# The edge phase's order keys replaced: where Pool's weights, VectorE's totals and comparisons stand in their queues

## What is computed

```
hi = x @ W1[:H];  hj = x @ W1[H:]
h = relu(hi[:, :, None, :] + hj[:, None, :, :] + b1)
y = layernorm(h @ W2 + b2) * gamma + beta
out = einsum('bij,bijh->bih', adj, y)
x = layernorm(x + out)
```

## Time and profile before

| | us |
|---|---|
| median of 3 runs | 449.18 (448.45 to 449.66) |
| the profiled launch, its time | 449.61 |
| its span, first to last instruction | 447.9 |
| TensorE (PE) busy | 429.5 |
| VectorE (DVE) busy | 422.7 |
| ScalarE (ACT) busy | 393.8 |
| Pool busy | 353.6 |

### The profile page before, as it was taken

The page is one execution under the profiler, slowest core; times in us unless marked ns, Lnnn a source line. Parts: engine busy times, 40 slices in busy tenths (PEclk is TensorE's granted clock), DMA queues, the critical chain, the costliest instruction groups (busy, mean ns, idle before and its releaser), DMA issues. The chain is left out here.

```text
span 447.9 us, 14059 instructions
## 1 busy us (share of the span) xinstructions
PE 429.5 (96%) x3391; PEld 403.8 (90%) x3391; DVE 422.7 (94%) x1555; ACT 393.8 (88%) x1001; POOL 353.6 (79%) x651
## 2 busy tenths in 40 slices
PE   7599989999999999999999999999999999999993
PEld 3599989999999999898999999999999999999992
DVE  6999999999999999998999999999999999999976
ACT  2378979999999899979899999999999999999994
POOL 3569979999999899953776878787878787878772
PEclk9989999999999999999999999999999999999998
DMA  6134334445444743232422223222323232323111
GB/s 225 43 86 124 101 127 159 154 157 159 155 157 152 240 162 120 80 129 78 136 89 73 88 66 92 66 92 64 94 64 94 64 94 63 95 65 97 59 37 50
DMA packets 50939, 47.60 MB, mean 106 GB/s; under 512 B 5584, under 2 KB 42576, under 8 KB 50896
## 3 DMA queue, kind: packets, MB, share of 16 engines
q1 hardware_dynamic: 49760, 46.45, 33.7%
q10 hardware_dynamic: 1136, 0.66, 0.5%
HBM read 28.22 MB, written 18.87 MB: 105 GB/s over the span
## 5 line engine op out<-in xcount | busy, mean ns | idle before, releaser
L1621 PE MATMUL bank<-w2c,hE 128*128 128x128 f32 x512 | 68.3, 277 | 0.4 <-ACT bank L928 0.4
L1621 PEld LDWEIGHTS bank<-w2c,hE 128*128 128x128 f32 x512 | 63.5, 192 | 2.6 <-issue 0.7
L1289 DVE TENSOR_TENSOR ym<-bank,wE 128x512 f32<-128x512 f32 x64 | 43.4, 684 | 4.3 <-POOL wE L775 3.3
L1264 DVE TENSOR_REDUCE ssum<-sqE 128x4 f32<-128x512 f32 x63 | 42.7, 678 | 3.0 <-ACT sqE L945 2.7
L1122 DVE BATCH_NORM_STATS2 stats<-t 128x6 f32<-128x128 f32 x192 | 44.5, 273 | 1.0 <-issue 1.0
L945 ACT ACTIVATE sqE<-bank 128x512 f32<-128x512 f32 x63 | 38.0, 603 | 8.0 <-PE bank L1621 8.0
L915 ACT ACTIVATE hE<-bank,front 128x512 f32<-128x512 f32 x64 | 43.5, 680 | 1.5 <-PE bank L1601 1.5
L742 POOL TENSOR_TENSOR half<-ym 128x512 f32<-128x512 f32 x31 | 39.6, 1276 | 5.7 <-DVE ym L1289 2.1
L775 POOL TENSOR_TENSOR wE<-erstd,fits 128x12 f32<-128x12 f32 x31 | 6.6, 213 | 44.8 <-DVE erstd L1278 44.8
L726 POOL TENSOR_TENSOR gHl<-gH,gHu 128x512 fp32r<-128x512 f32 x32 | 40.8, 1276 | 1.2 <-ACT gHu L899 1.2
L928 ACT ACTIVATE bank<-b2c 128x512 f32<-128x512 f32 x62 | 37.4, 604 | 0.5 <-DVE ym L1289 0.4
(11 more groups left out here) (192 smaller groups left out, 1643.6 us busy)
## 6 DMA issues: line engine op xcount, KB each, us to landing
hh_scratch<-hh SPq DMA_DIRECT2D x32, 256.0 KB, 2.2
gH<-hh_scratch SPq DMA_DIRECT2D x32, 256.0 KB, 2.7
A<-adj_groups SPq DMA_DIRECT2D x32, 128.0 KB, 2.1
res_scratch<-res SPq DMA_DIRECT2D x32, 128.0 KB, 2.0
gRES<-res_scratch SPq DMA_DIRECT2D x32, 128.0 KB, 2.0
AT<-adjT_groups SPq DMA_DIRECT2D x31, 128.0 KB, 2.2
out<-y SPq DMA_DIRECT2D x30, 128.0 KB, 1.8
X<-x_groups SPq DMA_DIRECT2D x29, 128.0 KB, 2.2
```

The source lines that it names most:

```text
L1264: nc.vector.tensor_reduce(ssum[q][:, g * ELL:(g + 1) * ELL], sqE[g][:, :, :], AX.X, ALU.add).then_inc(b[f"ssE{g}_ready"], 1)
L1289: nc.vector.tensor_tensor(ym[q][:, g, :, :], YE_ps[g], spread_last(wE[q][:, g * ELL:(g + 1) * ELL]), ALU.mult).then_inc(b[f"ymE{g}_ready"], 1)
L1621: last = nc.tensor.matmul(ps[:, i, :], hidden[:, i * P:(i + 1) * P], w2c[:, :], start=False, stop=i == tiles - 1, skip_group_check=seeded)
```

## The change

All keys of `T3` and `FIRST` get new values. No instruction is added, removed or altered, and no semaphore; only the order changes, on all engines' queues. Two of T3's five rows, cut:

```diff
@@ T3
-              "d1": 35.73, "dc": 35.41, "rec": 36.53, "x0": 40.69, "x1": 41.31, "yn": 41.92, "tot": 45.95, "st": 51.14, "ag": 51.41, "frec": 55.35,
-              "spl": 23.72, "hs": 25.25, "a1": 40.1, "a2": 42.41, "gm": 44.38, "rs": 45.6, "w": 35.72, "om": 52.88, "sh": 53.85}
...
+              "d1": 35.57, "dc": 35.42, "rec": 36.15, "x0": 37.73, "x1": 41.68, "yn": 41.53, "tot": 44.79, "st": 50.82, "ag": 51.05, "frec": 52.9,
+              "spl": 26.13, "hs": 18.2, "a1": 41.34, "a2": 43.84, "gm": 44.09, "rs": 48.79, "w": 35.79, "om": 55.35, "sh": 56.27}
```

More of the change, by code:

```diff
@@ L364, in wait_past @@
                 engine.wait_ge(semaphore, n)
-        T3 = {"idx": 18.98, "rows": 29.95, "V": 33.91, "cols": 36.46, "g0": 34.64, "g1": 38.22, "gc": 38.09, "m0": 38.25, "m1": 38.57, "mc": 38.29,
[4 rows of a table removed]
+        T3 = {"idx": 19.91, "rows": 32.14, "V": 34.14, "cols": 37.54, "g0": 37.07, "g1": 39.54, "gc": 39.53, "m0": 40.49, "m1": 41.12, "mc": 40.73,
[4 rows of a table added]
         AGES = 4
         START3, EARLY, CATCH = 216.0, 5.0, 25.0
-        FIRST = {("Qp", 0): 219.13, ("Qp", 1): 221.26, ("Qp", 2): 230.17, ("Qp", 3): 240.76, ("Qp", 4): 250.69, ("Qp", 5): 261.11, ("Qp", 6): 305.61,
[7 rows of a table removed]
[L383 to L386, removed]
[4 rows of a table removed]
-                 ("frec", 3): 354.98, ("frec", 4): 377.23, ("frec", 5): 433.5, ("frec", 6): 479.84, ("frec", 7): 597.74, ("fstd", 0): 255.59,
-                 ("fstd", 1): 272.03, ("fstd", 2): 304, ("fstd", 3): 307.1, ("fstd", 4): 329.45, ("fstd", 5): 360.71, ("fstd", 6): 387.64,
[6 rows of a table removed]
[L399 to L402, removed]
[8 rows of a table removed]
-                 ("rec", 0): 230.93, ("rec", 1): 243.38, ("rec", 2): 253.14, ("rec", 3): 266.15, ("rec", 4): 286.69, ("rec", 5): 371.3,
-                 ("rec", 6): 380.43, ("rec", 7): 395.56, ("rows", 0): 220.19, ("rows", 1): 225.18, ("rows", 2): 231.18, ("rows", 3): 252.04,
-                 ("rows", 4): 273.75, ("rows", 5): 312.4, ("rows", 6): 322.8, ("rows", 7): 347.8, ("rs", 0): 239.21, ("rs", 1): 252.36,
[8 rows of a table removed]
-                 ("sh", 7): 368.47, ("spl", 0): 212.77, ("spl", 1): 218.79, ("spl", 2): 225.48, ("spl", 3): 235.56, ("spl", 4): 245.46,
-                 ("spl", 5): 259.39, ("spl", 6): 312.86, ("spl", 7): 374, ("spu", 0): 183.55, ("spu", 1): 217.3, ("spu", 2): 226.04,
-                 ("spu", 3): 232.29, ("spu", 4): 244.95, ("spu", 5): 254.16, ("spu", 6): 270.1, ("spu", 7): 284.7, ("sqc", 0): 228.99,
-                 ("sqc", 1): 236.21, ("sqc", 2): 245.83, ("sqc", 3): 259.45, ("sqc", 4): 276.27, ("sqc", 5): 277.67, ("sqc", 6): 292.79,
-                 ("sqc", 7): 376.85, ("st", 0): 249.46, ("st", 1): 262.52, ("st", 2): 275.92, ("st", 3): 336.82, ("st", 4): 372.9, ("st", 5): 374.49,
-                 ("st", 6): 400.55, ("st", 7): 412.66, ("std", 0): 231.68, ("std", 1): 239.35, ("std", 2): 251.61, ("std", 3): 264.53,
-                 ("std", 4): 314.04, ("std", 5): 322.9, ("std", 6): 327.82, ("std", 7): 334.05, ("tot", 0): 245.11, ("tot", 1): 254.06,
-                 ("tot", 2): 265.45, ("tot", 3): 271.56, ("tot", 4): 320.85, ("tot", 5): 338.09, ("tot", 6): 360.32, ("tot", 7): 453.47,
[5 rows of a table removed]
@@ new lines, in gnn_stack @@
+        FIRST = {("Qp", 0): 220.01, ("Qp", 1): 221.02, ("Qp", 2): 228.66, ("Qp", 3): 242.33, ("Qp", 4): 249.12, ("Qp", 5): 263.93, ("Qp", 6): 325.5,
[7 rows of a table added]
+                 ("app", 0): 265.66, ("app", 1): 297.31, ("app", 2): 303.44, ("app", 3): 345.23, ("app", 4): 374.01, ("app", 5): 395.76,
+                 ("app", 6): 433.89, ("app", 7): 457.18, ("beg", 0): 220.15, ("beg", 1): 223.1, ("beg", 2): 226.74, ("beg", 3): 240.38,
+                 ("beg", 4): 252.17, ("beg", 5): 293.64, ("beg", 6): 304.76, ("beg", 7): 442.69, ("cols", 0): 224.51, ("cols", 1): 228.38,
+                 ("cols", 2): 240.52, ("cols", 3): 258.11, ("cols", 4): 280.11, ("cols", 5): 280.21, ("cols", 6): 296.34, ("cols", 7): 333.58,
[4 rows of a table added]
+                 ("frec", 3): 351.55, ("frec", 4): 368.2, ("frec", 5): 430, ("frec", 6): 472.29, ("frec", 7): 573.15, ("fstd", 0): 258.55,
+                 ("fstd", 1): 270.21, ("fstd", 2): 305.84, ("fstd", 3): 321.08, ("fstd", 4): 325.86, ("fstd", 5): 379.89, ("fstd", 6): 404.16,
[6 rows of a table added]
+                 ("idx", 0): 205.47, ("idx", 1): 219.81, ("idx", 2): 221.25, ("idx", 3): 231.44, ("idx", 4): 237.29, ("idx", 5): 258.08,
+                 ("idx", 6): 298.96, ("idx", 7): 351.8, ("kS", 0): 222.23, ("kS", 1): 226.48, ("kS", 2): 232.08, ("kS", 3): 246.52,
+                 ("kS", 4): 263.17, ("kS", 5): 288.84, ("kS", 6): 297.57, ("kS", 7): 453.18, ("kST", 0): 226.38, ("kST", 1): 229.63,
+                 ("kST", 2): 244.89, ("kST", 3): 258.45, ("kST", 4): 269.48, ("kST", 5): 281.25, ("kST", 6): 317.79, ("kST", 7): 322.16,
[8 rows of a table added]
+                 ("rec", 0): 230.18, ("rec", 1): 245.48, ("rec", 2): 253.66, ("rec", 3): 270.94, ("rec", 4): 290.45, ("rec", 5): 367.61,
+                 ("rec", 6): 386.74, ("rec", 7): 391.18, ("rows", 0): 220.28, ("rows", 1): 225.9, ("rows", 2): 229.85, ("rows", 3): 250.52,
+                 ("rows", 4): 272.76, ("rows", 5): 302.72, ("rows", 6): 316.63, ("rows", 7): 351.46, ("rs", 0): 243.54, ("rs", 1): 270.21,
[8 rows of a table added]
+                 ("sh", 7): 414.01, ("spl", 0): 211.63, ("spl", 1): 217.44, ("spl", 2): 228.89, ("spl", 3): 246.34, ("spl", 4): 254.81,
+                 ("spl", 5): 255.45, ("spl", 6): 330.83, ("spl", 7): 382.79, ("spu", 0): 188.86, ("spu", 1): 200.94, ("spu", 2): 227.1,
+                 ("spu", 3): 239.08, ("spu", 4): 245.29, ("spu", 5): 264.06, ("spu", 6): 264.62, ("spu", 7): 267.5, ("sqc", 0): 228.88,
+                 ("sqc", 1): 238.5, ("sqc", 2): 245.73, ("sqc", 3): 263.71, ("sqc", 4): 290.23, ("sqc", 5): 291.26, ("sqc", 6): 308.26,
+                 ("sqc", 7): 385.05, ("st", 0): 249.36, ("st", 1): 287.22, ("st", 2): 290.07, ("st", 3): 314.23, ("st", 4): 370.72,
+                 ("st", 5): 406.23, ("st", 6): 422.43, ("st", 7): 442.35, ("std", 0): 231.23, ("std", 1): 240.93, ("std", 2): 253.46,
+                 ("std", 3): 264.68, ("std", 4): 326.01, ("std", 5): 326.68, ("std", 6): 335.98, ("std", 7): 345.62, ("tot", 0): 247.39,
+                 ("tot", 1): 256.59, ("tot", 2): 277.75, ("tot", 3): 292.28, ("tot", 4): 327.06, ("tot", 5): 352.98, ("tot", 6): 366.8,
[5 rows of a table added]
```

## The result

The changed kernel takes 474.66 us (median of 4 runs, 474.09 to 474.80), the kernel before in the same comparison 449.06 us (4 runs, 448.45 to 449.66). The ratio is 1.0568, 95% interval 1.0549 to 1.0586: slower by 25.6 us, where the prediction said 28.3. The profiled launch took 474.74 us, with a span of 473.0.

A forecast was written before the change was run, and what follows sets the result against it. TensorE, VectorE and ScalarE were nearly full; the change closes a chain through VectorE and Pool. 8.23 plus 0.30 gives 8.53 us a turn; 27 turns make 230.3, minus 201.7, minus 0.5: +28.1, so 477.5 us, between 473 and 482.

The forecast's parts named there:

- tot: VectorE's total, first piece of each turn's chain: 0.36 us from start to end.
- tot to gamma: From tot's end on VectorE to gamma's start on an idle Pool: 0.08 us.
- gamma to wE: On Pool, from gamma's start to the start of the weights wE, which now follow it: 0.69 us.
- wE to ym: From wE's start on Pool to the start of VectorE's first weighing ym: 0.24 us.
- orstd to tot: On VectorE, from the short reciprocal orstd to tot: 0.13 us, taken as for erstd to tot.
- ym to erstd: VectorE's queue from the first ym to the next erstd: 6.76 us less 0.16, so 6.60, before the meeting.
- the meeting: VectorE's comparison starts amid Pool's residual tout and is held: 0.30 us more a turn, bounds 0 and 0.52.
- move of Qp: On VectorE, Qp fills the pause between the statistics' end and the aggregation: 0.16 us less a turn.
- The ends: First turn: 0 counted with 2 us of play; last turn: 0 to 1 us back, 0.5 taken.
- the rival's 483.5: Rival: the comparison starts only after tout ends, 0.52 more, 8.75 us a turn, 483.5 us; chance 0.10.
- hidden gamma: Rival: gamma fits Pool's idle stretch if tot ends over 0.7 us before erstd; turn 7.3, 445 us; chance 0.04.
- accE: Pool's accE, ready 7.01 us after wE, leaves 0.39 before tot; later accE or hs, above 486: chance 0.03.

The follow-up runs named there:

- w_first: The changed kernel with gamma and the weights exchanged again on Pool, so the weights wE come first: 449.75 us, ratio 1.0007.
- gamma_first: The kernel before with one key altered, so that gamma stands ahead of wE on Pool in the loop: 477.72 us, ratio 1.0623.
- rs_ahead: The changed kernel with Pool's residual tout also ahead of the weights, directly behind gamma, and SyncE's residual load moved earlier: 493.37 us, ratio 1.0998.
- tot_early: The changed kernel with tot moved ahead of T2 on VectorE and accE directly behind half on Pool: 462.62 us, ratio 1.0283.
- tot_early_x1: tot_early with the second ym ahead of yC again on VectorE: 463.44 us, ratio 1.0334.
- tot_x1_beg: tot_early_x1 with the comparison moved directly behind the deviations' reciprocals, into the hand-over: 455.46 us, ratio 1.0162.
- beg_in_gap: The changed kernel with the comparison moved behind tot and ahead of the first ym, into VectorE's hole: 470.57 us, ratio 1.0489.

## Why the prediction was right

The mechanism was the one predicted, and w_first and gamma_first show it from both sides. The terms of the sum follow, beside what the profile after shows. One more row of VectorE in the kernel before, the second sum of the turn of the earlier trace rows:

```profile
310.04 0.68 DVE L1270 TENSOR_REDUCE ssum<-sqC 128x4 f32<-128x512 f32 x1
```

- **tot**: 0.36 was taken, it takes 0.41. **tot to gamma** 0.08, **gamma to wE** 0.70, **wE to ym** 0.24: as predicted to 0.01.
- **orstd to tot** was taken as 0.13, as for erstd to tot. It is 0.02 (313.53 to 313.55), and orstd itself 0.10 where it was 0.15 in the earlier trace rows.
- **ym to erstd**, with the meeting, was to be 6.60 + 0.30 = 6.90 and is 6.75. The meeting's size was right: begun to its follower takes 0.86, where it was 0.55. The move of Qp was undersized: from the statistics' start to that of the second sum (L1270) it was 1.76 before (308.28 in the earlier trace rows to 310.04 above) and is 1.44 (310.17 to 311.61), 0.32 less instead of 0.16.
- Together these make 8.34 instead of 8.53, and 26 of the turns have a mean of 8.35. The first, out of the passage, is 9.45 (wE at 230.02 and 239.47), for which the prediction allowed 2 us and counted none. In it VectorE enters the loop, and yC starts 2.17 after ym, with 0.78 idle; w_first has the same 0.77 there and a first turn of 8.59. 26 x 8.35 + 9.45 is 226.6.
- **The ends** were to give 0.5 back and took 0.2: 474.74 - 449.61 is 25.1, the turns are 24.9.

So 3.0 us were predicted too much against the profiled launch: 4.7 in the 26 turns, less 0.9 for the first and 0.7 at the ends. The mis-sized terms are orstd to tot and the move of Qp.

The meeting itself came as the earlier trace rows have it: begun ended 0.41 after tout, as it had ended 0.40 after half. The Trainium skill's rule in "SBUF — State Buffer", section "Who interferes with whom", that the later one is fully blocked, would put the end 0.62 after tout and the whole at the rival's 483.5, an estimate; the trace agrees that the later one is held, but shows less than that price. What the prediction did not see is that a good third of this price was not the meeting's: in every second turn of the loop, 10 turns in all, the loop edge would have held yC for 0.29 in its place, as rs_ahead and w_first show. This cost the forecast nothing, because the edge lay under the meeting; had the two added up, 10 turns of 0.29 would have been 2.9 us more. That they did not is luck: the prediction knew nothing of the edge.

Of the rivals, "hidden gamma" named a condition (tot done 0.7 us ahead of erstd) and a price that the runs do not bear out: tot_early and tot_early_x1 met the condition, with tot's end 0.74 ahead of erstd's, and were 13 to 15 us slower than before. The prediction's 7.3 us for that case left out that tot also fills the hand-over, and the meeting. accE was nearer to being the bound than said: it ends at 313.41, 0.14 ahead of tot and not 0.39. It ends 7.01 after wE, as worked out; it is tot that starts earlier than said, 7.15 after wE. TensorE's share is 0.90, where seven eighths were foretold, and the clock is at 1.00 as foretold.

## What to carry to other kernels

When two engines hand work to each other once per turn, read both queues together: if what one engine waits for stands behind work whose input comes from the other engine's next step, the two waits add, and here a tie of two keys was enough for it. An instruction that lies inside a hand-over is cover; moved out, it costs its own length and leaves the wait bare. Before a gain from a shorter wait is counted, look for what is next in line (here the loop edge and another engine's squares).

## What the runs showed of the hardware that was not expected

- The loop edge costs VectorE time after a wait: a branch and eight register instructions stand behind the ym that waits, and the next computing instruction started 1.22 us after ym's start with nothing between (tot_x1_beg), 1.50 with the comparison between (rs_ahead), and 2.17, with 0.78 of it idle, where the loop is entered (changed kernel, unit 3). In the kernel before, 1.76 us of work lay there and it was not seen. Which part of the edge takes the time no run separates.
- Of a comparison and a Pool tensor_tensor that meet, the one on Pool can get longer too, but only a little. Where the comparison began first, gamma took 0.78 instead of 0.74 and wE behind it 0.26 instead of 0.21 (beg_in_gap); where tout began first, it took 0.73, no more than elsewhere (changed kernel).
- The hand-over from erstd's end to wE on Pool is 0.19 and 0.35 us in the two halves of the loop body, on an idle Pool.
